# The neighbourhood layer of a four-layer attention network: 19x19 surroundings instead of three row blocks

## The chip, the cores and the metric

The kernel runs on one core of a Trainium2 chip. The metric is the device time of one execution in microseconds (us). The core's engines are PE (TensorE, matrix products, with PEld for its weight loads), DVE (VectorE), ACT (ScalarE), POOL (GpSimd) and SP (SyncE, which here only issues DMAs). They run independent instruction streams in order and wait for each other through semaphores. PSUM is the memory that PE writes to, in banks of 512 float32 per partition; SBUF is the on-chip memory of all engines.

## What is computed

Eight images of 32x32 tokens with 192 channels run through four layers. Each normalises its input over channel groups, applies attention with 12 heads of 16 channels and adds the outcome to its input. Layers 0 and 2 add relative positions to the scores, layer 3 rotates q and k and adds a 5x5 convolution of v. Layer 1, the only one that the change touches, lets a query see the 7x7 tokens around it (moved inwards at the border) and 16 register tokens that all queries share:

```python
mask = make_neighbourhood_mask(7, 7, h, w)              # rows start_h..start_h+6 and columns start_w..start_w+6
mask_cat = jnp.concatenate([mask, jnp.ones((s, r), dtype=bool)], axis=-1)
scores = jnp.einsum('bnqe,bnke->bnqk', q, k_cat) * scale
scores = jnp.where(mask_cat[None, None], scores, NEG_INF)
attn = jax.nn.softmax(scores, axis=-1)
o = jnp.einsum('bnqk,bnke->bnqe', attn, v_cat)
return o.reshape(n, h, w, nh * e) @ out_w.T + out_b
```

`start_h` is `clip(h_pos - 3, 0, 25)`, so a query in the upper half of the image sees key rows 0 to 18 only, one in the lower half rows 13 to 31; columns likewise.

## The kernel before

`program` runs the layers one after another. For layer 1 it calls `normalise_block` and then `attend_block` with kind "window"; each is a block of its own, and the engines meet at its end.

`normalise_block` goes over the eight images: SP loads one (L126, L137), DVE takes statistics (L165) and writes the normalised image (L188), ACT writes input plus output bias (L259, L260), SP stores both (L141, L148). PE does one tiny product per image.

`attend_block` has 24 units: three groups of four heads, and in each the eight images. A unit has 32 tiles, a tile being 128 queries (four image rows, a chunk) of one head. The keys of a chunk are the 384 tokens of three neighbouring chunks and a block of 128 that holds the 16 registers and is masked otherwise: 512 keys (`KEYS_W`). Per tile

- `scores` (L782): q and k split into bf16 parts stacked to 96 rows, two products of 384 and 128 columns into one of four banks of `S`;
- `row_max` (L962, DVE): adds the mask, writes the negated sum to `PROB`, and its row maximum to `nmax`;
- `exponential` (L1043, ACT): exp of that tile in SBUF, with the row sum;
- `turn` (L799, PE): four 128x128 transposes into `PT`, then a copy of 512 columns to `PTS`, of even tiles by DVE (L973), of odd ones by ACT (L1054);
- `output` (L814, PE, once in four tiles): 16 products with V.

In the same streams, at fixed places t of the 32 tiles, stand the projections of the next unit's q, k and v (`job`, L445 and L460, all through the one PSUM bank `M`; DVE takes them out at L527, POOL splits q and k into three bf16 parts, SP moves these through DRAM into `KK` and `QQ`), and the tail of the last unit (`tail`: row sums inverted, spread and turned at L834, multiplied at L942, output projection at L843, copy at L1034, added to the stream in DRAM by POOL's DMA at L710). PE does not go on to the next job or tail before the last one's use of `M` is over (`prep_out`, `tail_out`). The loops over units are real loops for units 2 to 21, and every engine executes its instructions in the written order.

Rows of other layers are used below as prices. `attend_rot` (layer 3) has 96 units of eight steps, four heads and 256 queries each: per step eight transposes (L2402), ACT's exp straight out of PSUM (L2533) and a product of V in four column groups (L2413); every other step four score products (L2388); and a tail of a sum (L2425), an inverse (L2431) and the projection. `attend_rel` (layers 0 and 2) makes scores with rounded float32 operands (`F32R`) that occupy 64 of the array's 128 rows, in pairs (L1499, L1503, L1518, L1524).

## Time and profile before

| | us |
|---|---|
| runs without profile, median of three | 9050.09 |
| lowest and highest of them | 9038.95, 9065.04 |
| the profiled execution, own time | 9057.34 |
| its span, first to last instruction | 9055.6 |

The profiled execution lies 7 us above the median of the others. All times of the trace count from its first instruction. A view of instructions gives for a group its count and busy time; PE's durations contain the length of its pipeline, so that n products in a row take about n times their spacing plus one latency. "Idle before" names what released the engine. A stage in this text is one block of one layer. A float32 product appears as two records in the trace, each with its own weight load, a transpose and a rounded float32 (`F32R`) product as one.

### The profile page before, as it was taken

Reading aid. Unit: us, or ns where it says so; the run is one execution under the profiler, and the core shown is the slowest. Engines: PE = TensorE matmul, PEld = TensorE weight load, DVE = VectorE, ACT = ScalarE, POOL = GpSimd, SP = SyncE. Lnnn points to the kernel's source line nnn. Section 1 sums busy time; section 2 is a strip of 40 time slices with the busy share of each in tenths; the row PEclk is TensorE's granted clock in tenths of the full one; section 3 lists DMA queues with packets and bytes.
Section 4 is the critical chain, followed back from the end, with each engine's and each line's share of the span. In section 5 each row is a group of like instructions: output and inputs, shape, how many; then the busy total and the mean of one; then the engine's idle time right before and its main releaser. Section 6 shows DMA issues by size and latency. Waiting matters only on the chain. (4 is left out here: it accounts for less than half of the span.)

```text
span 9055.6 us, 188790 instructions
## 1 busy us (share of the span) xinstructions
PE 7343.7 (81%) x62744; PEld 4481.5 (49%) x62744; DVE 5241.4 (58%) x8043; ACT 4335.9 (48%) x8449; POOL 2240.3 (25%) x2715
## 2 busy tenths in 40 slices
PE   2999999989388777846998999899556499999998
PEld 2555555555155555534555555555222255555555
DVE  3655555556255555553555555555588666666665
ACT  1444444444265656541444444445111277777776
POOL 2343434343121211214343434332111000000000
PEclk7989999999698999976998999899777799999999
DMA  6757666766433334346767565764312254445443
GB/s 160 134 114 142 124 131 119 138 120 112 110 74 70 74 68 76 69 119 117 142 119 129 115 135 117 132 121 82 101 56 80 78 133 112 122 119 127 116 119 90
DMA packets 536711, 999.82 MB, mean 110 GB/s; under 512 B 102258, under 2 KB 303027, under 8 KB 500211
## 3 DMA queue, kind: packets, MB, share of 16 engines
q1 hardware_dynamic: 479346, 900.50, 45.7%
q0 software_dynamic: 56576, 88.90, 6.5%
q8 instruction: 484, 7.93, 0.4%
q14 instruction: 305, 2.49, 0.1%
HBM read 645.95 MB, written 335.81 MB: 108 GB/s over the span
## 5 line engine op out<-in xcount | busy, mean ns | idle before, releaser
L1676 DVE TENSOR_REDUCE a_nmp<-a_S 128x2 f32<-128x1024 f32 x1536 | 1878.2, 1224 | 1362.7 <-PE a_S L1524 1347.3
L1777 ACT ACTIVATE a_PROB<-a_T 128x512 f32<-128x512 f32 x3072 | 1667.6, 595 | 1959.9 <-PE a_T L1503 1949.0
L1373 POOL CAST a_RF<-a_RL 32x512 fp32r<-32x512 f32 x1536 | 1295.0, 843 | 1120.8 <-DVE a_RL L1704 1028.8
L2492 DVE CUSTOM_DVE_ANT_0 a_X<-a_S,a_mask 128x1024 f32<-128x1024 f32 x768 | 910.0, 1223 | 551.9 <-PE a_S L2388 548.5
L1499 PE MATMUL a_T<-a_QW,a_KW 64*128 64x512 f32 x3072 | 813.4, 522 | 300.4 <-issue 135.3
L2533 ACT ACTIVATE a_PROB<-a_T 128x512 f32<-128x512 f32 x1536 | 835.8, 601 | 382.9 <-PE a_T L2402 382.9
L1499 PEld LDWEIGHTS a_T<-a_QW,a_KW 64*128 64x128 f32 x3072 | 313.8, 193 | 1312.3 <-issue 1309.3
L1537 PE MATMUL a_O<-a_PROB,a_V 128*32 128x512 f32 x6144 | 929.5, 681 | 2.5 <-ACT a_PROB L1777 2.5
L2402 PE MATMUL a_T<-a_ident,a_X 128*128 128x128 f32 x6144 | 824.7, 277 | 101.8 <-DVE a_OSB L2509 98.1
L962 DVE CUSTOM_DVE_ANT_0 a_PROB<-a_S,a_mask 128x512 f32<-128x512 f32 x768 | 522.8, 688 | 591.9 <-PE a_PT L799 498.4
L2402 PEld LDWEIGHTS a_T<-a_ident,a_X 128*128 128x128 f32 x6144 | 671.8, 141 | 303.0 <-issue 285.3
L1524 PEld LDWEIGHTS a_S<-a_KV,a_QV 64*128 64x128 f32 x6144 | 662.2, 203 | 124.2
L1518 PE MATMUL a_S<-a_KW,a_QW 64*128 64x512 f32 x3072 | 674.6, 427 | 55.1 <-issue 28.5
L1524 PE MATMUL a_S<-a_KV,a_QV 64*128 64x256 f32 x6144 | 667.2, 293 | 0.0
L1503 PE MATMUL a_T<-a_QV,a_KV 64*128 64x512 f32 x3072 | 657.9, 416 | 0.0
L2553 ACT ACTIVATE a_X<-a_X,a_rmax 128x512 f32<-128x512 f32 x768 | 564.6, 735 | 57.6 <-DVE a_rmax L2492 57.6
L1043 ACT ACTIVATE a_PROB<-a_PROB,a_nmax 128x512 f32<-128x512 f32 x768 | 550.5, 720 | 77.7 <-DVE a_nmax L962 77.7
L2343 POOL DMA_DIRECT2D out<-a_Y x96 | 92.0, 959 | 1805.0 <-ACT a_PROB L2533 1794.8
L799 PE MATMUL a_PT<-a_ident,a_PROB 128*128 128x128 f32 x3072 | 487.7, 283 | 50.4 <-ACT a_PROB L1043 30.3
L1564 PE MATMUL a_T<-a_QC,a_tab_d 16*32 16x64 f32 x6144 | 413.0, 300 | 138.3 <-issue 103.4
L2413 PE MATMUL a_O<-a_PROB,a_V 128*32 128x256 f32 x6144 | 491.1, 391 | 15.7 <-ACT a_OSB L2541 11.3
L2146 DVE SCALAR_TENSOR_TENSOR n_CV<-n_VP,n_lw,n_CV 96x1024 f32<-96x1024 f32 x384 | 461.0, 1275 | 0.0
(158 smaller groups left out, 9847.0 us busy)
## 6 DMA issues: line engine op xcount, KB each, us to landing
a_QV<-a_part_rows SPq DMA_DIRECT2D x384, 256.0 KB, 7.2
a_rel_rows<-a_RF SPq DMA_DIRECT2D x96, 1024.0 KB, 9.2
a_K<-part_rows SPq DMA_DIRECT2D x576, 128.0 KB, 4.0
a_X<-xn_scratch SPq DMA_DIRECT2D x72, 768.0 KB, 6.7
stream<-a_Y POOLq DMA_DIRECT2D x288, 192.0 KB, 4.6
a_part_rows<-a_part SPq DMA_DIRECT2D x48, 1024.0 KB, 12.2
a_QV<-a_part_rows SPq DMA_DIRECT2D x384, 128.0 KB, 7.8
a_QV<-a_rel_rows SPq DMA_DIRECT2D x384, 128.0 KB, 6.4
```

The lines of the kernel that those rows point to most:

```text
L1373: nc.gpsimd.tensor_copy(dst, src).then_inc(permuted, 1)
L1499: nc.tensor.matmul(T[:, slot(("st", s, pr, sd))], KW[lines, keys], QW[lines, par, pr, cols], start=True, stop=False)
L1503: nc.tensor.matmul(T[:, slot(("st", s, pr, sd))], KV[lines, par, pr, keys], QV[lines, par, pr, kc // 2, cols], start=False, stop=True).the ...
L1518: nc.tensor.matmul(S[:, pr, sd], QW[lines, par, pr, queries], KW[lines, kh * BANK:(kh + 1) * BANK], start=True, stop=False)
L1524: last = nc.tensor.matmul(S[:, pr, sd, here], QV[lines, par, pr, 2 * kh + kq, queries], KV[lines, par, pr, keys], start=False, stop=kq == 1)
L1537: last = nc.tensor.matmul(O[Q * g:Q * g + Q], V[:, par, kc, g], PROB[:, s % PRING, g], start=kc == 0, stop=kc == CHUNKS - 1)
L1676: nc.vector.tensor_reduce(nmp[:, qh, c, 2 * pr:2 * pr + 2, kh], S[:, pr], AX.X, ALU.max).then_inc(s_done, 1)
L1777: nc.scalar.activation(PROB[:, s % PRING, 2 * pr + sd], T[:, slot(("st", s, pr, sd))], ACT.Exp).then_inc(t_act, 1)
L2402: last = nc.tensor.transpose(T[:, slot(("t", kc, p)), P * (2 * sd + c):P * (2 * sd + c) + P], X[:, par, c, 2 * p + sd, P * kc:P * kc + P], ...
L2492: nc.vector.tensor_tensor_reduce(out=X[:, v % 2, c, g], in0=S[:, sd].rearrange("p a b -> p (a b)"), in1=mask[:, n % 2, g, c], scale=1.0, s ...
L2533: nc.scalar.activation(PROB[:, kc % PRING, 2 * p:2 * p + 2].rearrange("p g x -> p (g x)"), T[:, slot(("t", kc, p))], ACT.Exp, scale=-1.0). ...
L2553: nc.scalar.activation(here, here, ACT.Identity, scale=-1.0, bias=rmax[:, par, c, 2 * p + 1:2 * p + 2]).then_inc(x_act[half], 1)
```

## The change

`normalise_block` and `attend_block` are replaced, for layer 1, by `prepare_win` and `attend_win`; `attend_block` is gone. Layers 0, 2 and 3 keep their code.

The image is cut into quarters of 16x16 queries. A quarter's queries see only the 19x19 tokens in the corner of the image next to them. `prepare_win` goes over the images once. It normalises as before (DVE), then POOL gathers the four 19x19 surroundings with the registers in between into `XG` (4 x 384 tokens). PE projects q for all heads from the image and k and v from the gathered copy; q and k leave PSUM through DVE (bias, scale), ACT rounds them to `F32R`, DVE subtracts to get the rest, and SP stores both parts as `q_rows`, `k_rows`, `v_rows` in DRAM. The input is copied to the stream by eight DMAs from DRAM to DRAM. Everything is written out, without loops.

`attend_win` has 24 units again (four heads of one image), each with four quarters ("turns") of three key chunks of 128: 12 steps. A score is one `F32R` product over 79 rows: three times 16 rows of q and k parts, then 18 and 13 rows which hold the mask in factored form: one-hot rows on the query side for its place in rows and in columns, and on the key side 0 or -2^100; and two rows with the negated row maximum in two parts. Scores are made twice. Queries on partitions (`straight`), two tiles of 128 queries, four heads, only as many columns as these queries can see, for the row maximum, which DVE reads out of PSUM; and keys on partitions (`transposed`), 256 queries, for ACT's exp out of PSUM straight into `PROB`, so that nothing has to be transposed before the product with V. V has 16 columns of ones, which bring the row sums. The maxima are turned by PE two at a time (`turn_max`) and written by DVE into rows 64 and 65 of `Q_` (`take_max`).

```diff
-def attend_block(nc, sems, name, kind, xn, stream, w, ident):
+def attend_win(nc, sems, name, stream, w, ident, q_rows, k_rows, v_rows, near_lines):
+    UNITS = GROUPS * IMAGES
+    QUADS, CHUNKS_N = 4, NEAR // P
+    STEPS = QUADS * CHUNKS_N
+    RING, PRING, BUFS = 3, 3, 3
+    ROWS = 3 * DIM + 16 + 2 + 13
+    SPANS = {(0, 0): (0, 256, 0, 226), (0, 1): (94, 284, 0, 284), (1, 0): (0, 284, 0, 284), (1, 1): (128, 256, 24, 226)}
+    ITEMS = {0: (0, 1), 1: (2,), 2: (3,)}
+    TAIL = {2: "sum", 3: "turn0", 5: "turn1", 6: "wo00", 8: "wo01", 9: "wo10", 11: "wo11"}
+    NM_AT = 1
...
+            for u in range(UNITS):
+                for s in range(STEPS):
+                    quad, kc = divmod(s, CHUNKS_N)
+                    t = QUADS * u + quad
+                    transposed(u, s, 0)
+                    transposed(u, s, 1)
+                    if t + 2 < TURNS_N:
+                        for i in ITEMS[kc]:
+                            straight(t + 2, i)
+                    if s:
+                        values(u, s - 1)
+                    elif u:
+                        values(u - 1, STEPS - 1)
+                    if kc == NM_AT and t + 1 < TURNS_N:
+                        turn_max(t + 1)
+                    if u and s in TAIL:
+                        tail(TAIL[s], u - 1)
...
+            def row_max(t, i):
+                nc.vector.tensor_reduce(nm[:, t % 2, tile, 2 * pr:2 * pr + 2], S[:, n % 2, :, at:at + width], AX.X, ALU.max,
+                                        negate=True).then_inc(s_done, 1)
...
+            def take_max(t):
+                for g in range(G):
+                    last = nc.vector.tensor_copy(Q_[64:66, u % BUFS, g, WIDE * quad:WIDE * quad + WIDE],
+                                                 T[Q * g:Q * g + 2, slot(n), 0:WIDE])
...
+            def exponential(u, s, pr):
+                nc.scalar.activation(PROB[:, (STEPS * u + s) % PRING, 2 * pr:2 * pr + 2].rearrange("p g x -> p (g x)"),
+                                     T[:, slot(n)], ACT.Exp).then_inc(t_act, 1)
...
-        normalise_block(nc, sems, f"n{i}", x, xn, streams[i], w["bo"], a["gavg"])
-        if kind == "rel":
+        if kind == "window":
...
+            prepare_win(nc, sems, f"n{i}", x, streams[i], w, a["gavg"], q_rows, k_rows, near_rows, near_lines)
+            attend_win(nc, sems, f"a{i}", streams[i], w, a["ident"], q_rows, k_rows, near_rows, near_lines)
+        else:
+            normalise_block(nc, sems, f"n{i}", x, xn, streams[i], w["bo"], a["gavg"])
             attend_rel(nc, sems, f"a{i}", xn, streams[i], w, a["ident"])
```

The work is new code rather than moved code, so the order of two engines shows it best. TensorE in the attention of layer 1, before, four tiles in the middle of a unit's tail (`a_S` scores, `a_PT` transposes, `a_O` the product with V, `a_M` the output projection):

```order
L799 MATMUL a_PT<-a_ident,a_PROB 128x128 x4
L843 MATMUL a_M<-a_OSB,a_wo 96x512
L782 MATMUL a_S<-a_KK,a_QQ 128x384
L782 MATMUL a_S<-a_KK,a_QQ 128x128
L799 MATMUL a_PT<-a_ident,a_PROB 128x128 x4
L814 MATMUL a_O<-a_PTS,a_V 16x128 x16
L782 MATMUL a_S<-a_KK,a_QQ 128x384
L782 MATMUL a_S<-a_KK,a_QQ 128x128
L799 MATMUL a_PT<-a_ident,a_PROB 128x128 x4
L843 MATMUL a_M<-a_OSB,a_wo 96x512
```

The same engine now, three steps of a unit with two parts of the tail (`a_T` from `a_Q`,`a_K` the turned scores, `a_S` the straight ones, `a_T` from `a_nm_wide` the turned maxima):

```order
L798 MATMUL a_T<-a_Q,a_K 128x256 x4
L784 MATMUL a_S<-a_K,a_Q 128x256 x4
L813 MATMUL a_O<-a_PROB,a_V 32x256 x4
L847 MATMUL a_T<-a_OSB,a_wo 96x512
L798 MATMUL a_T<-a_Q,a_K 128x256 x4
L784 MATMUL a_S<-a_K,a_Q 128x284 x2
L813 MATMUL a_O<-a_PROB,a_V 32x256 x4
L823 MATMUL a_T<-a_ident,a_nm_wide 128x128 x2
L798 MATMUL a_T<-a_Q,a_K 128x256 x4
L784 MATMUL a_S<-a_K,a_Q 128x284 x2
L813 MATMUL a_O<-a_PROB,a_V 32x256 x4
L847 MATMUL a_T<-a_OSB,a_wo 96x512
```

The transposes of the probabilities are gone; each group of turned scores stands before the straight scores of two turns later and the product with V of the step before.

VectorE in the same stage, before: the masked maximum of each tile (its two rows are one call) and the copies of turned tiles.

```order
L962 ISA a_PROB,a_nmax<-a_S,a_mask 128x512
L962 ISA a_nmax 128x1
L973 COPY a_PTS<-a_PT 128x512
L962 ISA a_PROB,a_nmax<-a_S,a_mask 128x512
L962 ISA a_nmax 128x1
```

VectorE now, one turn and the start of the next:

```order
L887 TENSOR_REDUCE a_nm<-a_S 128x2 x3
L903 CAST a_Q<-a_T 2x256 x4
L887 TENSOR_REDUCE a_nm<-a_S 128x2
L893 CAST a_nm_hi<-a_nm 128x8
L895 COPY a_nm_wide<-a_nm_hi 128x8
L896 TENSOR_TENSOR a_nm_wide<-a_nm,a_nm_hi 128x8
L911 RECIPROCAL a_inverse<-a_T 128x32
L913 COPY a_inverse_wide<-a_inverse 128x1024
```

It has four reductions of two heads, four casts of two partitions and three small operations per turn, and the inverse of the row sums once in a unit.

## Rows read from the trace of the kernel before

**Rows 1.** The page's first line and its list of engines over the span.

```profile
span 9055.6 us, 188790 instructions
PE 7343.7 (81%) x62744; PEld 4481.5 (49%) x62744; DVE 5241.4 (58%) x8043; ACT 4335.9 (48%) x8449; POOL 2240.3 (25%) x2715
```

**Rows 2.** Timeline (start, us, operation): layer 1 begins, last store, attention begins, layer 2.

```profile
2360.21 0.34 SPq L121 DMA_DIRECT2D n_bias<-L_bo  x1
...
2435.75 0.32 SPq L148 DMA_DIRECT2D stream<-n_stream  x1
...
2442.78 0.37 SPq L577 DMA_DIRECT2D a_ident<-ident  x1
...
3985.64 0.34 SPq L121 DMA_DIRECT2D n_bias<-L_bo  x1
```

**Rows 3.** Stretch, length, busy time of each engine (count), TensorE's granted clock, DMA share, GB/s.

```profile
2360.00:2443.00 83.00, 3.83 (x16) 3.16 (x16) 40.99 (x113) 17.49 (x16) 5.62 (x9) 0.50 0.73 228
2443.00:2492.00 49.00, 20.27 (x40) 7.55 (x41) 3.49 (x9) 2.76 (x7) 8.47 (x12) 0.50 0.46 93
2492.00:3976.00 1484.00, 1199.28 (x12081) 778.44 (x12079) 844.84 (x2177) 906.73 (x2202) 286.46 (x396) 0.93 0.37 70
...
6383.00:7160.00 777.00, 415.62 (x1040) 192.44 (x1040) 612.64 (x660) 88.07 (x144) 98.20 (x68) 0.71 0.24 76
7160.00:9055.00 1895.00, 1687.16 (x14976) 1055.65 (x14976) 1248.88 (x2208) 1352.03 (x2496) 92.03 (x96) 0.99 0.48 118
```

**Rows 4.** Uses of the tile a_mask: ns min/median/max, first and last start in us.

```profile
L962 DVE CUSTOM_DVE_ANT_0 a_PROB<-a_S,a_mask x768: 679/691/693, 2491.2 to 3963.2; 128x512 f32<-128x512 f32 x192
L2492 DVE CUSTOM_DVE_ANT_0 a_X<-a_S,a_mask x768: 1219/1223/1225, 7182.0 to 9026.0; 128x1024 f32<-128x1024 f32 x192
```

**Rows 5.** Costliest groups from 2492 to 3976: busy us, mean ns, idle before and releasers.

```profile
L962 DVE CUSTOM_DVE_ANT_0 a_PROB<-a_S,a_mask 128x512 f32<-128x512 f32 x767 | 522.1, 688 | 576.2 <-PE a_PT L799 498.4 <-PE a_S L782 57.7 <-issue 19.8
L799 PE MATMUL a_PT<-a_ident,a_PROB 128*128 128x128 f32 x3072 | 487.7, 283 | 50.4 <-ACT a_PROB L1043 30.3 <-DVE a_PTS L973 16.6 <-issue 1.9
L445 PE MATMUL a_M<-a_X,a_wv 96*64 96x512 f32 (+1 forms) x276 | 129.5, 600 | 109.2 <-DVE a_whole L527 109.2
L843 PE MATMUL a_M<-a_OSB,a_wo 128*96 128x512 f32 x192 | 100.9, 607 | 62.5 <-DVE a_OSB L942 61.7 <-ACT a_Y L1034 0.8
```

**Rows 6.** Timeline of PE in layer 0's attention: start, busy us, operation, count.

```profile
1503.25 0.39 PE L1518 MATMUL a_S<-a_KW,a_QW 64*128 64x512 f32 x2
...
1503.48 0.40 PE L1524 MATMUL a_S<-a_KV,a_QV 64*128 64x256 f32 x4
...
1503.80 1.98 PE L1545 MATMUL a_T<-a_X,a_wqk 96*128 96x512 f32 x4
...
1505.72 0.50 PE L1499 MATMUL a_T<-a_QW,a_KW 64*128 64x512 f32 x2
```

**Rows 7.** Timeline of layer 3's attention: start, busy us, operation, count.

```profile
8001.92 0.64 PE L2413 MATMUL a_O<-a_PROB,a_V 128*32 128x256 f32 x8
...
8002.49 1.09 PE L2402 MATMUL a_T<-a_ident,a_X 128*128 128x128 f32 x8
...
8008.77 0.61 PE L2425 MATMUL a_T<-a_pick,a_OSB 128*128 128x4 f32 x4
```

**Rows 8.** Groups by line over the whole span, as prices for DVE and ACT.

```profile
L1676 DVE TENSOR_REDUCE a_nmp<-a_S 128x2 f32<-128x1024 f32 x1536 | 1878.2, 1224 | 1362.7 <-PE a_S L1524 1347.3
L2533 ACT ACTIVATE a_PROB<-a_T 128x512 f32<-128x512 f32 x1536 | 835.8, 601 | 382.9 <-PE a_T L2402 382.9
...
L2509 DVE TENSOR_TENSOR a_OSB<-a_OSB,a_T 128x256 f32<-128x256 f32 x96 | 39.9, 415 | 2.9 <-PE a_T L2431 2.9
...
L1683 DVE CAST a_nm_hi<-a_nm 128x16 fp32r<-128x16 f32 x96 | 29.6, 309 | 3.3
```

**Rows 9.** Timeline at the start of layer 3's preparation: first load, first large product.

```profile
6383.28 0.34 SPq L1926 DMA_DIRECT2D n_X<-stream  x1
...
6404.19 9.81 PE L2023 MATMUL n_T<-n_XN,n_wv 96*96 96x512 f32 x16 [3.30 <-DVE n_XN L2095]
```

More of the change, by code:

```diff
@@ L469, in add_v_jobs @@
-        def add_v_jobs(step, halves):
-            for i, half in enumerate(halves):
-                job(step + 2 * i, project(wv_sb, G * DIM, half), act=[v_out(half)])
-                run, place = turn_v(half)
-                job(step + 2 * i + 1, run, act=[place])
-        def free_whole(n, piece):
-            before = UNIT_STEPS * n + SPLIT_STEPS * piece - (REL_STEPS if piece == 0 else 0)
-            need(nc.vector, split, before, solo=True)
-            if rel:
-                need(nc.vector, moved, 16 * G * (PIECES * n + piece), solo=True)
@@ L571, in attend_block @@
+        CONSTS = 16 * (len(const) + 1)
+        SETUP = 5
+        NORM = 10
+        GATHERS = 2 * QUADS
         block = ctx.enter_context(nc.Block())
@@ L785, in turn @@
-            def turn(u, t):
-                T = TILES * u + t
-                pe.wait_ge(exp_done, T + 1)
-                for h in range(TURNS):
-                    bank = t % 2 if window else h
-                    if window:
-                        need(pe, evac_act if t % 2 else evac_dve, EVACS * u + t // 2)
-                    else:
-                        need(pe, evac_act if h else evac_dve, T)
-                    alone(pe)
-                    for j in range(4):
-                        k = BANK * h + P * j
-                        last = nc.tensor.transpose(PT[:, bank, P * j:P * j + P], PROB[:, t % PROBS, k:k + P], ident_sb[:])
-                    last.then_inc(turned, 1)
@@ L903, in _ @@
+            pe.wait_ge(consts_loaded, CONSTS)
+            pe.wait_ge(set_up, SETUP)
+            alone(pe)
+            mean(0)
+            for b in range(IMAGES):
+                for i, n in enumerate(ORDER):
+                    job(b, n)
+                    if i == FIRST_MEAN and b + 1 < IMAGES:
+                        mean(b + 1)
         @block.vector
         def _(eng):
-            def scale_k(n):
-                eng.wait_ge(loaded, 16 * LOADS * (n + 1))
-                for ap in scaled:
-                    last = nc.vector.tensor_scalar(ap, ap, SCALE, None, ALU.mult)
-                last.then_inc(w_scaled, 1)
@@ L1018, in _ @@
+            rest(NP * IMAGES - 1)
         @block.scalar
         def _(act):
[L1020 to L1034 removed]
@@ L1081, in epilogue, with high @@
-            def epilogue():
-                n = UNITS - 1
-                outputs(n, 1)
-                tail(n, 1, 1)
-                tail(n, 1, 2)
-            pairs(act, prologue, body, epilogue)
+            act.wait_ge(consts_loaded, CONSTS)
+            act.wait_ge(set_up, SETUP)
+            alone(act)
+            def high(n):
+                b, i = divmod(n, NP)
+                what, m, at = PIECES[i]
+                act.wait_ge(t_dve, n + 1)
+                if at == 0:
+                    need(act, (q_stored if what == "q" else k_stored)[m], 16 * b)
+                alone(act)
+                if what == "q":
+                    ins = nc.scalar.copy(q_part[:, m, 0, at * BANK:(at + 1) * BANK], whole[:, n % BLOCKS])
+                else:
+                    ins = nc.scalar.copy(k_part[:, m, 0, at], whole[:, n % BLOCKS, 0:NEAR])
+                ins.then_inc(hi_done, 1)
@@ new lines, in values @@
+            def values(b, j):
+                s = b % 2
+                act.wait_ge(t_ready, done(b, ("v", j, 0), "pe"))
+                if j == 0:
+                    need(act, v_stored[s], 16 * (b // 2))
+                alone(act)
+                nc.scalar.copy(VT[:, s, 2 * j:2 * j + 2, :, 0:DIM],
+                               T[:, ORDER.index(("v", j, 0)) % RING, 0:2 * CHANNELS].rearrange(
+                                   "p (c h d) -> p c h d", c=2, d=DIM)).then_inc(t_act, 1)
+            for b in range(IMAGES):
+                for n in ORDER:
+                    if n[0] == "v":
+                        values(b, n[1])
+                    else:
+                        high(NP * b + PIECES.index(n))
```

1222 lines of the change are left out of this document (574 added, 648 removed).

## The prediction

> **What bounds the kernel now.** I read first the list of engines [rows 1]: TensorE (PE) is busy for 81% of the span and nothing else is near. That is an average over eight stages, and the change touches two, so the second view is the three starts [rows 2]: layer 1 runs from 2360.2 to 3985.6, 1625.4 us. Its normalisation takes 82.6 of them, its attention 1542.9. The third view is the table by stage [rows 3]. In the normalisation PE does nothing and DMA has a share of 0.73. In the first 49 us of the attention PE is at the lower clock. In the long stretch PE is busy for 1199 of 1484 us with a granted clock of 0.93, DVE for 845, ACT for 907.
>
> The use of the mask gives the period: 768 tiles in 1472 us, 1.92 us a tile, 61.4 us a unit [rows 4]. The groups say who waits: DVE sat idle 498 us until PE's transposes were over [rows 5]. PE in turn waited 109 us at the v projection for DVE to empty the only bank `M`, and 62 us at the output projection for the product in `OSB` [rows 5]. So PE's in-order stream ends last: its work, plus handovers in the stream. The prices below give 1.7 us of PE work a tile (four transposes 0.56, two score products 0.4, a quarter of the V product 0.25, projections and tail 0.5) against 1.92. What counts for the change is PE's work per unit.
>
> **Prices of PE records at 2.4 GHz.** A float32 product of 512 columns: four records from 1503.80 to 1505.72 [rows 6], less 0.2 for the change of group, 0.43 each, 0.84 ns a column. A rounded float32 product: a pair of 512 columns in the two halves of the array passes in 0.23 (1503.25 to 1503.48), and four of 256 in 0.32 as two pairs (to 1503.80) [rows 6]; so 0.115 for 256 columns and 0.1 for a change of group. The V product of layer 3 (four column groups, 256 columns, two records each) takes 0.57 with its change (8001.92 to 8002.49) [rows 7]; the new one has the same shape. A transpose: (1.09 - 0.28)/7 = 0.116, with the 283 ns of one as latency [rows 5, 7]. A product of four columns, where only the weight load counts: (0.61 - 0.26)/3 = 0.117, with about 0.26 for one, my estimate [rows 7].
>
> The new scores take 79 rows, so they can't run in pairs side by side: each of them pays its 0.115 alone. The Trainium skill ("TensorEngine Tiling (Array Packing)", Key Properties) has a rule against the new order: a change of tiling mode drains the engine, and each step goes from the full array to 32-column groups and back. By the row the whole V group, change included, is 0.57, of which 0.43 are its columns, so no more than 0.14 is lost [rows 7]. The sum would be 0.2 us a step more if a drain of a whole latency came at each change; layer 3's row has both changes in it and doesn't show that.
>
> **Attention, per step.**
> - Turned scores: 4 x 0.115 and two changes, 0.66.
> - Straight scores: 8/3 products of 256 or 284 columns at 0.12 and a change, 0.42.
> - V product 0.57. Two transposes of maxima in three steps, 0.11.
> - Tail per unit: sum 16 x 0.117 = 1.87, turns 8 x 0.116 = 0.93, projection 8 x 0.43 = 3.44, seven changes 0.7; 6.94/12 = 0.58.
>
> Together 2.34 us. The same prices on layer 3 give 2.24 (transposes 1.13, V 0.57, scores 0.28, tail 0.26); measured are 95 units of eight steps in 1844 us, 2.43 [rows 4]. A finished pipeline of this kind thus loses 0.19 a step to handovers and to its clock (0.99 [rows 3]); with 0.11 for the new one, whose DVE and ACT are less loaded, I take 2.45 us. Bounds: 2.25 if the changes of group cost less and no wait is left, 2.9 if the waits double those of layer 3 and the clock is granted at 0.93 as now [rows 3]. The work of 288 steps: 706 us (648 to 835).
>
> Does another engine end later? ACT: two exps of 512 columns at 0.60 [rows 8], a third of an output copy of 256 columns and a third of a projection copy of 512, which by their columns cost 0.3 and 0.6 like an exp: 1.5. DVE per turn: four reductions of 452 or 568 elements. By elements of the 1024-wide one (1.22) they cost 0.61, by a fixed share at most 0.75: 2.4 to 3.0. Four casts of two partitions by 256: no row shows them; between the 0.31 of a 16-element cast and the 0.42 of a 256-wide product from PSUM, 1.2 to 1.7 [rows 8]. The small split 0.9. With a tail of 2.3 a unit that is 1.7 to 2.05 a step. Both lie under 2.45, and hide behind PE. If PE were faster than 2.05, DVE would be next. The dangerous wait is take_max: after PE turns two maxima, DVE has 1.7 us of casts, and PE comes to the turned scores that need them one step (2.4) later. PE would stand 0.3 us or so a turn if casts took 0.6. DMA: 2.7 MB of operands and 0.8 MB of stream per 29 us, 120 GB/s, as in layer 3 (118 at share 0.48 [rows 3]), issued two units ahead: hidden.
>
> **Preparation, per image.** q: 32 records of 256 columns, 6.9 us; k: 32 of 384, 10.3; v: 72 of 192, 11.6; 18 changes of group 1.8. That is 30.7 us of PE, 31 with the tiny product of the means, at full clock. It replaces 10 us an image of normalisation and takes the projections out of the attention. DVE has about 21 us (statistics and normalisation 5.1 as now, 40.99 us for eight images [rows 3], then 12 copies out of PSUM and 12 subtractions at 0.5 to 0.8), ACT 9, POOL some 5 for the gathers, which start 8 us before their use. The stores and loads are 7.1 MB an image, at the 228 GB/s of the normalisation [rows 3] 31 us too; its share was 0.73, so 23 us if more is possible. So 31 us (29 to 38), eight images 248 (232 to 304).
>
> Around it: from first load to first large product 20.9 us in layer 3's preparation [rows 9]; I take 21, since the memsets of POOL are of the same size. After the last product 9 us of evacuation and stores, and 8 of block change (now 7 between the last store at 2435.75 and 2442.78 [rows 2]). Start of the attention: 18 constant loads, then operands, the first scores and maxima, 27. End: last tail, last store and block change 25, where now 22 lie between the last masked maximum (3963.2 [rows 4]) and the next layer.
>
> **Sum.** 21 + 248 + 17 + 27 + 706 + 25 = 1044 us against 1625.4 [rows 2]: 581 saved. Layers 0, 2 and 3 keep their time. The span 9055.6 becomes 8475, the profiled execution 9057.3 becomes 8476, and on the median's base 9050.1 - 581 = 8469; I say 8470.
>
> **Rivals.**
> 1. Handovers and DVE decide (12%): casts on two partitions cost 0.6, PE stands for the maxima, a step takes 2.85. For it: it is the one chain through PE, DVE and PE with one step of air. Against: DVE has 0.4 to 0.7 us a step to spare. 288 x 0.4 = 115 more: 8585.
> 2. The preparation runs at the lower clock (7%): in all short stages of now the grant is 0.50, in layer 3's preparation 0.71 [rows 3]. For it: PE there waits for ring slots and for the next image. Against: these stages have PE busy for 5 to 53% of the time, here it would be dense. At 1.2 GHz 30 us an image more, 240: 8710.
> 3. No waits left (5%): 2.2 us a step, 8398.
> 4. Slower than before (3%): both new stages stay at the lower level for good. The 40% busy first 49 us of the attention had it [rows 3]. The preparation pays 240, a step of 2.34 becomes 4.7, 288 x 2.25 = 648 more: 9358. The point from which it decides is a step of 4.47 us, with the preparation as forecast; with the preparation at 1.2 GHz 3.6 us. Against it: 0.93 and 0.99 in the two stages with PE as busy as here.
> 5. DMA bounds the preparation (3%): 36 to 40 us an image, 8530.
> That the transposes stay in some form is excluded by the order of instructions: none of `PROB` is left.
>
> **Chances.** My forecast, step 2.3 to 2.65 and image 29 to 35 us, has 70%; its own range is 8410 to 8560. The range for 8 in 10 takes in rival 3 and 5 and most of 1, and the bounds of step (-58, +129) and image (-16, +56): low 8390, high 8640. Rival 2 and 4 stay out. A difference of 0.3%, 27 us, is what a measurement of this kernel can tell from none. Faster by more than that: all but rival 4, 97%. Within it 1%, slower 2 to 3%.
>
> **What would show it.** In the changed profile the layer starts at 2360 and ends near 3404. PE's products with V in it should come 2.45 us apart, 29 us a unit; waits of the turned scores for `a_Q` casts would show rival 1; DVE busy under 2 us a step. In the preparation q's first products come every 31 us and the clock is above 0.9; below 0.7 is rival 2; idle of DVE or ACT on `q_rows`, `k_rows` or `v_rows` is rival 5. Wrong from the start would be the prediction if a product of 79 rows in `F32R` has not the 0.115 us of a paired one: at twice that a step takes 3.1 us, 8660.

## The result, and the profile after

The changed kernel takes 8731.6 us (median of four, 8712.5 to 8750.1) against 9046.4 us before: a ratio of 0.965, interval 0.9632 to 0.9666. It is faster by 315 us, as forecast in sign; forecast were 580 us, and the time lies above the range's end of 8640. The profiled execution took 8719.0 us, its span 8717.3. Of the 338 us between the two spans 291 are layer 1; the rest lies in code that did not change.

The page of the kernel after, its first line and its engines, answers [rows 1]:

```profile
span 8717.3 us, 168356 instructions
PE 7201.7 (83%) x56896; PEld 4389.3 (50%) x56896; DVE 5013.6 (58%) x7203; ACT 3870.8 (44%) x7137; POOL 2200.3 (25%) x2407
```

PE's share has gone up and its work down by 142 us only. The starts of its four parts (timeline of the kernel after: start, busy us, operation) answer [rows 2]; the third row is the groups of turned scores, with their durations and first and last start:

```profile
2355.25 0.34 SPq L369 DMA_DIRECT2D n_X<-stream  x1
2789.18 0.34 SPq L711 DMA_DIRECT2D a_ident<-ident  x1
L798 PE MATMUL a_T<-a_Q,a_K x1152: 274/283/1202, 2853.1 to 3665.5; 79*128 79x256 f32 x192
3689.23 0.35 SPq L122 DMA_DIRECT2D n_bias<-L_bo  x1
```

Layer 1 now takes 3689.2 - 2355.3 = 1334 us where it took 1625.4 and was forecast at 1044. The missing 290 us are all in it. (What lies behind layer 1, unchanged code, took 5028 us against 5070 before; in the profiled executions of the twelve runs below that part lies between 5001 and 5055. Differences of that size are no effect of an edit, and the experiments are read from layer 1 first and from the whole time second.)

The stages (windows of the kernel after: stretch, length, busy time of PE, PEld, DVE, ACT, POOL with their counts, granted clock, DMA share, GB/s) answer [rows 3]. They are the preparation, the start of the attention, and its long stretch:

```profile
2355.00:2791.00 436.00, 354.83 (x1104) 218.04 (x1104) 152.29 (x305) 73.31 (x144) 49.92 (x85) 0.72 0.44 148
2791.00:2853.00 62.00, 5.09 (x18) 4.22 (x19) 6.02 (x14) 0.00 (x0) 0.00 (x0) 0.50 0.96 134
2853.00:3680.00 827.00, 712.78 (x5168) 464.63 (x5166) 505.05 (x1139) 388.31 (x768) 18.61 (x24) 0.87 0.52 99
```

Against the terms of the forecast, in us (an image is the spacing of the first `XN` of each, a step that of the first turned score of each, both from their starts in the trace):

| | forecast | after | too low by |
|---|---|---|---|
| preparation, to the first `XN` and product | 21 | 28 | 7 |
| eight images | 8 x 31 = 248 | 8 x 48.84 = 391 | 143 |
| end of it and block change | 17 | 15 | -2 |
| start of the attention | 27 | 63.9 | 37 |
| steps (288 forecast, 287 spacings measured) | 706 (2.45 each) | 811.9 (2.83 each) | 106 |
| end | 25 | 24 | -1 |

Three terms hold the miss, and each has waits in the trace that the prediction did not have. Waits of the preparation, DVE (who waits for what: us in all, times, longest):

```profile
DVE n_stats L514 <- DMA n_X<-stream: 82.5, 7, 12.2
DVE n_near_round L556 <- DMA n_near_drawn<-L_near: 37.0, 1, 37.0
```

The statistics of seven images wait some 12 us each for the image itself. The SP queue and DVE around one of them (timeline: start, busy us, operation, in brackets the idle time before):

```profile
2535.80 0.38 SPq L399 DMA_DIRECT2D near_rows<-n_VT  x1
2536.27 1.80 SPq L382 DMA_DIRECT2D n_X<-stream  x1
2552.81 2.47 DVE L514 BATCH_NORM_STATS2 n_stats<-n_X 96x6 f32<-96x512 f32 x4 [12.15 <-DMA n_X<-stream]
```

The load of the next image stands on SP behind the last store of the one before, is issued 0.5 us after it, and lands 16.5 us later. While DVE waits, PE runs dry, and what it does next is slow. A group of four records of the k projection in the first image and after the wait (PE's timeline):

```profile
2394.14 1.45 PE L485 MATMUL n_T<-n_XG,n_wk 96*96 96x384 f32 x4
2556.84 2.84 PE L485 MATMUL n_T<-n_XG,n_wk 96*96 96x384 f32 x4 [0.18 <-DVE n_whole L571]
```

At the start of the attention SP itself waits, with q and k of all units queued behind it; the second row is the median landing of one of its twelve loads of mask rows:

```profile
SPq L41 <- DMA a_K<-near_lines: 30.9, 1, 30.9
a_K<-near_lines SPq DMA_DIRECT2D x3, 360.0 KB, 21.9
```

In the steps, PE's waits from 2845 to 3660 are:

```profile
PE a_O L813 <- issue: 43.3, 71, 1.1
PE a_T L847 <- DVE a_Q L903: 26.1, 43, 0.9
PE a_O L813 <- ACT a_OSB L963: 17.3, 23, 0.8
PE a_T L834 <- DVE a_Q L903: 14.5, 23, 0.6
PE a_T L841 <- DVE a_Q L903: 7.5, 12, 0.6
...
PE a_T L798 <- DVE a_Q L903: 0.6, 1, 0.6
```

There are two waits in each turn: one at the V product, in part put down to ACT's copy of the output; and one of 0.6 us at whichever tail product stands at kc = 2 (the sum, turn 1, two projections), for the casts of `take_max`. The forecast's dangerous wait, turned scores for these casts, occurs once (last row). And the clock: 0.87 on average, but not evenly. PE in a unit with its tail (timeline; `L834` are the 16 records of the sum's eight products):

```profile
3120.45 0.64 PE L813 MATMUL a_O<-a_PROB,a_V 128*32 128x256 f32 x8 [0.75 <-ACT a_OSB L963]
3121.02 0.44 PE L823 MATMUL a_T<-a_ident,a_nm_wide 128*128 128x128 f32 x2
3121.21 0.72 PE L798 MATMUL a_T<-a_Q,a_K 79*128 79x256 f32 x4
...
3123.36 1.92 PE L834 MATMUL a_T<-a_pick,a_OSB 128*128 128x4 f32 x16 [0.63 <-DVE a_Q L903]
...
3127.68 1.20 PE L798 MATMUL a_T<-a_Q,a_K 79*128 79x256 f32 x4
```

and the windows around it: the sum alone, then 8 us behind it.

```profile
3123.30:3125.20 1.90, 1.83 (x17) 1.87 (x17) 1.00 (x4) 0.00 (x0) 0.00 (x0) 1.00 1.01 171
3126.00:3134.00 8.00, 7.78 (x48) 5.07 (x48) 5.62 (x13) 3.27 (x7) 0.00 (x0) 0.55 0.98 213
```

In the sum PE shows no gap and has the full clock. Soon after it the clock is at 1.2 GHz for most of 8 us, although PE is busy for 7.78 of them. Over the 24 units, the share of time at the lower level by step (0 to 11) is 0.04, 0.04, 0.15, 0.59, 0.65, 0.48, 0.33, 0.16, 0.12, 0.04, 0, 0: it starts behind the sum in step 2 and is under 0.2 from step 7 on.

### The profile page after: what moved, and what is told of

It is laid out like the page before. It is cut to its first block and busy times, and to the rows that moved or that the text cites. A ratio compares the mean times of both kernels' runs of the same rounds, so it can differ in the third digit from the quotient of the medians.

```text
span 8717.3 us, 168356 instructions
## 1 busy us (share of the span) xinstructions
PE 7201.7 (83%) x56896; PEld 4389.3 (50%) x56896; DVE 5013.6 (58%) x7203; ACT 3870.8 (44%) x7137; POOL 2200.3 (25%) x2407
## 5 line engine op out<-in xcount | busy, mean ns | idle before, releaser
L1681 ACT ACTIVATE a_PROB<-a_T 128x512 f32<-128x512 f32 x3072 | 1667.6, 595 | 1924.8 <-PE a_T L1407 1911.8
L2437 ACT ACTIVATE a_PROB<-a_T 128x512 f32<-128x512 f32 x1536 | 835.7, 601 | 382.2 <-PE a_T L2306 382.2
L954 ACT ACTIVATE a_PROB<-a_T 128x512 f32<-128x512 f32 x576 | 323.9, 597 | 371.3 <-PE a_T L798 371.3
L1468 PEld LDWEIGHTS a_T<-a_QC,a_tab_d 16*32 16x32 f32 x6144 | 359.1, 125 | 184.4 <-issue 166.8
L1608 DVE TENSOR_TENSOR a_RL<-a_T,a_RL 128x512 fp32r<-128x512 f32 x192 | 132.5, 690 | 452.3 <-ACT a_RL L1698 452.2
```

Of the source, the lines that this page charges most:

```text
L1468: last = nc.tensor.matmul(T[at + 32:at + 64, to, 64 * a:64 * a + 64], tab_d[:, x], QC[:, :, half * BANK + x:(half + 1) * BANK:SIDE], start ...
L1681: nc.scalar.activation(PROB[:, s % PRING, 2 * pr + sd], T[:, slot(("st", s, pr, sd))], ACT.Exp).then_inc(t_act, 1)
L2437: nc.scalar.activation(PROB[:, kc % PRING, 2 * p:2 * p + 2].rearrange("p g x -> p (g x)"), T[:, slot(("t", kc, p))], ACT.Exp, scale=-1.0). ...
```

## Experiments

Each kernel has the changed kernel as its base. Ratios are against the kernel before on the same chip; the changed kernel has 0.965. "The clock" of a stretch is the mean granted clock as a share of 2.4 GHz, 0.5 being 1.2 GHz throughout.

### The load of the next image

```diff
+            sp.dma_start(X[:, 1], x_in[1]).then_inc(x_loaded[1], 16)
...
-                if b + 1 < IMAGES:
-                    need(sp, xn_ready, 2 * b)
+                if b + 2 < IMAGES:
+                    sp.wait_ge(xn_ready, 2 * b + 2)
                     alone(sp)
-                    sp.dma_start(X[:, (b + 1) % 2], x_in[b + 1]).then_inc(x_loaded, 16)
+                    sp.dma_start(X[:, b % 2], x_in[b + 2]).then_inc(x_loaded[b % 2], 16)
```

> The preparation's load of the next image but one is issued as soon as its buffer is free, ahead of the stores of q, k and v, instead of behind the stores of the image before. Theory (the load waits in the queue behind 5.9 MB of stores, DVE waits for it, and PE with DVE): DVE's wait for n_X falls from 82.5 us to under 5, an image takes 31 to 37 us instead of 49.0, the granted clock of the stage rises from 0.72 to over 0.85, and the kernel gets 85 to 140 us faster than the changed kernel (8732), to about 8620. Rival (the DMA engines are full, the stores only wait elsewhere): DVE or ACT wait for q, k or v stores instead, an image stays over 44 us, the gain is under 35 us. Second rival (the clock stays low although the wait is gone): an image takes 42 to 45 us, gain 30 to 50 us.

Measured: 8600.9 us, 0.950 (0.9473 to 0.9522). The preparation took 315.3 us instead of 433.9, an image 33.1. Its window, beside the one of the kernel after above:

```profile
2350.00:2667.00 317.00, 272.15 (x1104) 174.54 (x1104) 153.26 (x305) 74.77 (x144) 51.88 (x85) 0.93 0.60 203
```

No wait of the statistics is left. The load itself is no faster: it still stands behind a `v_rows` store and lands after 16.5 us (median), but it is now issued an image ahead of its use. The same 1104 records of PE take 272 us instead of 355: 83 of the 119 us are the clock (0.72 to 0.93), which the wait had cost in addition to itself. DMA moves 203 GB/s in this window instead of 148, so its rate had not been the limit (rival 5).

### What lowers the clock in a unit

The first kernel makes the row sums for two of the eight chunks of queries only, each with its four columns four times, and leaves the other six out, so its row sums are wrong.

```diff
-                    for c in range(CHUNKS):
-                        last = nc.tensor.matmul(T[:, to, G * c:G * c + G], OSB[:, o, P * c:P * c + P], pick_sb[:],
+                    for c in range(2):
+                        last = nc.tensor.matmul(T[:, to, 16 * c:16 * c + 16].rearrange("p (r g) -> p r g", g=G), OSB[:, o, P * c:P * c + P],
```

> Left out: six of the eight products that bring the row sums to the other side in each unit; the two that stay write 16 columns each, so that all other steps run as before with wrong sums. 24 units lose 12 records of 0.117 us, 34 us. Theory (the 1.9 us of full weight loads with four columns behind them bring PE's clock down for the steps behind): the share of the lower clock in steps 3 to 6 of a unit, now 0.33 to 0.65, falls below 0.2, the clock of the stage rises from 0.87 to over 0.93, a unit gets 3 us or more shorter, the kernel 70 to 100 us faster than 8732. Rival (the clock follows the waits or the mix of the whole stage): it stays at 0.87, the gain is 30 to 40 us.

Measured: 8644.9 us, 0.954 (0.9523 to 0.9554). A step takes 2.52 us, the clock of the steps is 0.971, and steps 3 to 6 are at the lower level for 4% of their time. But work was removed with it: 12 of 16 records, 1.3 us in each of 23 units, some 31 of the 89 us by which the steps became shorter.

The second kernel keeps all of the work and gives it more: the same eight products move their four columns sixteen times, 64 columns each.

```diff
-                        last = nc.tensor.matmul(T[:, to, G * c:G * c + G], OSB[:, o, P * c:P * c + P], pick_sb[:],
-                                                start=True, stop=True)
+                        last = nc.tensor.matmul(T[:, to, 64 * c:64 * c + 64].rearrange("p (r g) -> p r g", g=G), OSB[:, o, P * c:P * c + P],
+                                                pick_sb[:].unsqueeze(1).to_broadcast([P, 16, G]), start=True, stop=True)
```

> The eight products of the row sums keep their weights and their number, but each moves 64 columns instead of 4 (the four wanted ones repeated 16 times); DVE reads the first four of each 64. Nothing is left out. Weight loads still set their pace (0.117 us a record), so the stretch stays at 1.9 us. Theory that the clock falls because almost no columns move in this stretch: the share of the lower clock in steps 3 to 5 falls below 0.25, clock of the stage over 0.93, step 2.55 to 2.7 us instead of 2.83, 40 to 80 us faster than the changed kernel (8732 to 8746 by its ratio). Rival (it falls because of the stretch's length with nothing but weight loads, or the 0.6 us wait in front): share stays at 0.6, time within 10 us.

Measured: 8638.0 us, 0.954 (0.9518 to 0.9554); step 2.63, clock 0.972. PE in a unit of this kernel, the sum and the second turned scores behind it:

```profile
3076.78 1.97 PE L834 MATMUL a_T<-a_pick,a_OSB 128*128 128x64 f32 x16 [0.63 <-DVE a_Q L903]
...
3080.72 0.72 PE L798 MATMUL a_T<-a_Q,a_K 79*128 79x256 f32 x4
```

The sum takes nearly as long as before (1.97 against 1.92, although sixteen times the columns pass), the wait before it is the same 0.63, and the turned scores that took 1.20 take 0.72. PE waits as often as before at the V product and more often for the casts (90 times instead of 78). So neither the wait nor the sum's length by itself lowers the clock: the two kernels differ in how many columns pass behind each weight load, 4 or 64, and only the one with 4 loses it. Numbers between were not tried. It is worth 0.203 x 287 = 58 us in the steps. (Layer 1 is 71 us shorter and the whole time 94; 11 of it came from the preparation, which this edit doesn't touch.) The Trainium skill ("TensorE: Matmul & The Clock Gate", Part 1) says the gate goes by how busy PE has recently been; by the trace's busy time the two kernels are the same there, and only one loses its clock, so the busy time of a profile does not tell which will.

A way around it without wider products is to make the sum in two parts, in steps 0 and 2:

```diff
-    TAIL = {2: "sum", 3: "turn0", 5: "turn1", 6: "wo00", 8: "wo01", 9: "wo10", 11: "wo11"}
+    TAIL = {0: "sum0", 2: "sum1", 3: "turn0", 5: "turn1", 6: "wo00", 8: "wo01", 9: "wo10", 11: "wo11"}
```

> The eight products of the row sums in two parts of four, in step 0 (first half of the tokens) and step 2 of a unit, with their own inverses. PE's work is the same. If the clock falls because of one long stretch of weight loads, two of 0.9 us with dense products between leave it up: share of the lower clock under 0.2 everywhere, step 2.5 to 2.6, 65 to 90 us faster than the changed kernel. If what counts is how much of such work a unit has, the share stays near 0.2 on the average, and the time within 20 us.

Measured: 8752.0 us, 0.965 (0.963 to 0.9679); step 2.91, clock 0.83, share at the lower level 0.23, 0.37, 0.63, 0.7, 0.6, 0.45 in steps 1 to 6. Half the stretch is enough to lose the clock, and there are two of them. The gain that was expected from shorter stretches did not come; the time is that of the changed kernel, as the other case had it.

### ACT's copy of the output

ACT copies the output of a turn after the first exp of step kc = 1. It goes to kc = 0, behind both exps:

```diff
                     exponential(u, s, 0)
-                    if s % CHUNKS_N == 1 and t:
-                        outputs(t - 1)
                     exponential(u, s, 1)
+                    if s % CHUNKS_N == 0 and t:
+                        outputs(t - 1)
```

> ACT copies the finished output of a turn one step part earlier, right behind the exps in whose step PE finishes it, instead of behind the next step's first exp. PE's first product with V of a turn then has nothing to wait for. Theory (these waits are on the path): the 0.75 to 0.9 us before the first V product of each of 96 turns go, 50 to 75 us faster than 8732, steps 1 of each turn 2.0 us instead of 2.5 to 2.9. Rival (PE then waits elsewhere, for the casts of the maxima): under 20 us.

Measured: 8642.0 us, 0.954 (0.9496 to 0.9574). A step takes 2.53 us; the steps with kc = 1 fell from medians of 2.50, 2.91, 2.89 and 2.80 to 1.67, 2.51, 2.00 and 2.00. PE's waits from 2850 to 3577, all rows there are:

```profile
PE a_T L847 <- DVE a_Q L903: 21.3, 45, 0.6
PE a_T L834 <- DVE a_Q L903: 13.7, 22, 0.6
PE a_T L841 <- DVE a_Q L903: 13.1, 21, 0.6
```

All waits at the V product are gone, those of "issue" too: 71 and 23 in the list above are 94, about one for each turn, so the row "issue" was the same wait. The edit is worth 0.296 x 287 = 85 us, more than the 60.6 us of these waits, and the waits for the casts stayed at 48. The rest came with the clock (0.894 over the steps instead of 0.871, some 55 us less at the lower level, which by its half speed is worth up to 27). Steps 3 and 4 are still at the lower level for 0.59 and 0.68 of their time, so this wait is not what lowers the clock; but in steps 5 and 6 the share fell from 0.48 and 0.33 to 0.13 and 0.08, so without the wait the clock comes back sooner. The V product waits for the copy of the turn before because the two turns use the two halves of one bank (`O` is 2 x 256 float32); what a bank for each would bring was not tried.

### The casts of the maxima and the ring slot

`turn_max` takes one of three slots of `T`, and it is free again after four casts. The tail product that stands behind it at kc = 2 needs that slot. Here the tail goes ahead of the maxima, and all of its parts but the last to kc = 0 or 1; DVE's stream follows the same order:

```diff
-    TAIL = {2: "sum", 3: "turn0", 5: "turn1", 6: "wo00", 8: "wo01", 9: "wo10", 11: "wo11"}
+    TAIL = {3: "sum", 4: "turn0", 6: "turn1", 7: "wo00", 9: "wo01", 10: "wo10", 11: "wo11"}
...
-                    if kc == NM_AT and t + 1 < TURNS_N:
-                        turn_max(t + 1)
                     if u and s in TAIL:
                         tail(TAIL[s], u - 1)
+                    if kc == NM_AT and t + 1 < TURNS_N:
+                        turn_max(t + 1)
```

> Six of the seven parts of the tail stand in the first and second step of a turn, ahead of the turned maxima, so that they no longer wait for the ring slot that the four casts of the maxima hold. Theory (this slot is the wait at the tail in every third step): PE's waits for the casts (26 + 14.5 + 7.5 us, and the same time again in weight loads) go, 25 to 45 us faster than 8732, more if the clock rises. Rival (PE comes to the turned scores that need the casts sooner and waits there): the same time is lost in front of the turned scores, gain under 10 us or a loss of up to 30.

Measured: 8775.0 us, 0.967 (0.9635 to 0.9706); step 3.04, clock 0.776: the steps behind the sum are at the lower level for 0.91, 0.98 and 0.96 of their time. The casts' waits fell from 48 us to 15, and the loss of clock took more: the time rose by 43 us, beyond both expectations. Why the clock falls deeper here than in the changed kernel stays open. It says nothing yet on the order itself; that comes below, on a base where the clock holds.

### The two starts

DVE rounds the mask rows after the first image's normalisation instead of before, and the mask rows are loaded buffer by buffer, each ahead of the unit that needs it:

```diff
             eng.wait_ge(consts_loaded, CONSTS)
-            nc.vector.tensor_copy(near_round[:], near_drawn[:]).then_inc(near_rounded, 1)
             statistics(0)
...
             normalise(0)
+            eng.wait_ge(near_stored, 16)
+            nc.vector.tensor_copy(near_round[:], near_drawn[:]).then_inc(near_rounded, 1)
...
-            for s in range(BUFS):
+            def mask_rows(s):
                 for lines, n, at in ((y_rows, 16, 0), (x_rows, 15, 16)):
...
-                    sp.wait_ge(consts_loaded, CONSTS)
+                    mask_rows(s)
+                    sp.wait_ge(consts_loaded, CONSTS + 16 * 4 * s)
```

> The rows of the mask are rounded and stored after image 0 is normalised, and the attention's three buffers get their mask rows one after the other, each followed by its operands, so that the first unit waits for four of the twelve row loads and its own operands alone. Expected from the trace of the changed kernel: first normalised image 21 us after the stage's begin instead of 28, first turned scores 30 to 40 us after the attention's begin instead of 64; together 30 to 40 us faster. Rival (all loads share the same engines and the first unit waits for the sum of them): first turned scores still after 50 us, gain under 20 us.

Measured: 8710.4 us, 0.962 (0.9587 to 0.9657). The first `XN` comes 16.8 us after the start instead of 28.0, the first turned scores 40.8 us after the start of the attention instead of 63.9: 34 us in the two, which is what the trace shows. The whole time fell by 21, and the two intervals of the ratio overlap, so it does not show the gain clearly. The first q and k now go out 16.3 us after the start of the attention, the first straight scores come 15.7 us later, and from there to the first turned scores it is 8.8 us.

### All of it

The first kernel has the early image, the early copy, the sum in two parts and the two starts.

> The early load of the images, the early copy of outputs, the sums in two parts and the later mask rows together. If their causes are apart the gains add: 137 for the image load, 85 to 100 for the copy, 65 to 90 for the sums, 30 to 40 for the starts, of which the clock's share can be won once only: step 2.2 to 2.3 us, layer 1 about 1040 to 1080 us instead of 1336, the kernel at 8420 to 8490. If they overlap (the copy's waits and the sum's stretch bring the clock down together) the step stays at 2.4 and the kernel over 8500.

Measured: 8473.0 us, 0.936 (0.9345 to 0.9376); layer 1 takes 1071.7 us, a step 2.46 at a clock of 0.93. The time is as expected for gains that add, the step is not (2.2 to 2.3 expected): PE still waits 48 us for the casts, and the clock is not full. The second has the wide sum in place of the one in two parts:

> The early load of the images, the early copy of outputs, the later mask rows and the sums with 64 moving columns in one part. Theory (the short columns of the sums are what brings the clock down, and nothing else in this stage does): low share under 0.1 in all steps, clock 0.97, step 2.40 us, which is the mean of the steps 0 to 11 as the runs with the early copy and with wide columns each had them; layer 1 1050 to 1070 us, the kernel at 8440 to 8470. Rival (the early copy makes another stretch light and the clock falls there): step over 2.5, no faster than 8473.

Measured: 8432.6 us, 0.930 (0.9282 to 0.9313). It computes everything and is the fastest of those that do. Layer 1 takes 1054.8 us: 304.5 for the preparation, 41.1 for the start of the attention, 686.4 for the steps (2.39 each, clock 0.96) and 23 for the end.

On this base the tail was moved ahead of the maxima, with the same edit as above:

> As the kernel with all four and wide sums, and six of the seven parts of the tail before the turned maxima, as in the run in which that alone cost time. Theory (there it lost only through the clock, and the wait for the ring slot that the casts hold is real, 0.4 to 0.6 us in four steps of a unit): with the clock up it gains 1.2 to 2 us a unit, step 2.25 to 2.3, the kernel 30 to 45 us faster than its companion. Rival (the turned scores then wait for the casts instead): the same time within 10 us, PE idle before the turned scores.

Measured: 8458.4 us, 0.933 (0.9315 to 0.9348), a step 2.43. The clock now stays (0.968), and the order brings nothing (26 us more than its companion, 12 of them in the steps): the waits go to the turned scores, which take the same slots one place later. The longest of PE's waits in this kernel:

```profile
PE a_T L803 <- DVE a_Q L908: 25.2, 46, 0.6
PE a_T L803 <- ACT a_Y L982: 9.7, 28, 0.4
PE a_T L803 <- DVE a_OSB L924: 9.5, 23, 0.4
```

The last pair asks what the casts still cost, by making only the first of the four, beside the same kernel with all of them. Three heads of four then subtract stale maxima, and the result is wrong:

```diff
-                for g in range(G):
+                for g in range(1):
                     last = nc.vector.tensor_copy(Q_[64:66, u % BUFS, g, WIDE * quad:WIDE * quad + WIDE],
```

> All the edits of e9_all_wide, and of the four casts that store the maxima's two rows of the four heads only the first is made; the rows of the other three heads stay as they were, so three heads of four subtract wrong maxima. It asks what the casts still cost when the rest is mended: four of them take about 1.7 us a turn on VectorE, one takes 0.43, so each turn has 1.3 us less between the reductions and the next products that want their slot. Theory (the casts are the last wait left on the way): TensorE's waits before the turned scores, the tail products and the weight-load products for a_Q go, and the step falls from 2.39 to about 2.2, some 45 us less than e9_all_wide. Rival (TensorE's own work and its handovers from line to line are what is left): the step stays within 0.05 us of 2.39 and the time within 15 us of e9_all_wide.

> The same kernel as e9_all_wide, on the same chip as e11_one_cast, so that the two are compared side by side: 8433 us within 20, step 2.39 us.

Measured: 8410.8 us (0.929, 0.9261 to 0.931) with one cast, 8434.5 us (0.933, 0.9304 to 0.9356) with four; a step takes 2.227 against 2.392. PE's waits in the stretch of the steps, first with four casts (the first three rows), then with one (all rows there are):

```profile
PE a_T L852 <- DVE a_Q L908: 20.5, 44, 0.5
PE a_T L846 <- DVE a_Q L908: 14.1, 23, 0.6
PE a_T L839 <- DVE a_Q L908: 13.7, 22, 0.6
```

```profile
PE a_S L789 <- DMA a_Q<-near_lines: 4.9, 1, 4.9
PE a_T L803 <- issue: 1.4, 1, 1.4
PE a_S L789 <- issue: 0.5, 1, 0.5
PE a_O L818 <- issue: 0.4, 1, 0.4
```

The 48.3 us of waits are gone and the steps are 47.3 us shorter: the theory holds in the trace. The tail products read nothing that the casts write, so what they waited for is the slot. The whole time fell by 24 us only, between the two expectations; in the profiled executions layers 2 and 3 took 54 us more than in the kernel beside it (5054.7 against 5000.6), which is as far apart as that part ever was. The window of the steps with one cast shows what is left:

```profile
2701.00:3335.00 634.00, 626.85 (x5081) 410.44 (x5081) 379.85 (x849) 388.81 (x753) 17.35 (x22) 0.95 0.69 132
```

PE is busy for 99% of it, at a clock of 0.95. 2.2 us a step is PE's own work.

## Why the prediction was right and wrong

**Right: the sign, PE's prices and what hides behind PE.** Where no wait falls and the clock is full, steps 0, 3, 6 and 9 of the kernel after take 2.06, 2.16, 2.23 and 2.55 us (medians), and with nearly all waits removed the mean of all steps is 2.23, against a sum of prices of 2.34. The 79-row product is not twice the price of a paired one: four with their changes take the 0.56 from 3121.21 to the next group at 3121.77, forecast were 0.66. The drain at each change of tiling mode, which would have made it 2.54, is in no row. (The price of being wrong there was set too low: twice the time for both kinds of scores adds 0.46 + 0.32 us, a step of 3.2 and about 8690, not 3.1 and 8660.) DVE's reductions took 0.63 and 0.75, as bounded, its work is 1.75 us a step (505 us in 288 steps), ACT's 1.35; both hide. DMA hides behind the steps (share 0.52). End and block change were right within a microsecond or two.

**Wrong: the image, 31 us, measured 48.8.** The work was right: with the load early an image takes 33.1. The failed step is the bound on transfers, "The stores and loads are 7.1 MB an image, at the 228 GB/s of the normalisation [rows 3] 31 us too; its share was 0.73, so 23 us if more is possible". That was a rate; what counted was the place of one load in SP's order. `x_in[b + 1]` stands behind the `v_rows` store of image b - 1, and that store waits for the last of ACT's work on it. So the load is issued when its image is already due, and lands behind a store of 2.3 MB after 16.5 us. The Trainium skill ("DMA: Bandwidth & Descriptors", Queues, rings and completion order) says that on each DMA engine the descriptors of a queue are consumed in ring order; the trace agrees: the load issued 0.5 us behind that store, whose own median landing is 14.0 us, lands last. It would have been enough to walk SP's order in the kernel. PE's gaps that go with it are 36 us in all (436.0 - 354.8 against 317.0 - 272.2); rival 2 came on top of it, for the reason that the forecast named ("PE there waits for the next image") and then set aside with the word "dense". The clock was 0.72, as in layer 3's preparation (0.71 [rows 3]), the nearest row; for the full clock that the forecast took there was no row. It cost 83 us, a third of rival 2's price, since the clock came back within each image.

**Wrong: the start of the attention, 27 us, measured 63.9.** It was costed as a count of loads. The twelve loads of mask rows (3.7 MB) hold up SP for 30.9 us before the first q and k go out. DMA in that stretch (window of the kernel after):

```profile
2792.00:2828.00 36.00, 0.00 (x0) 0.00 (x0) 0.00 (x0) 0.00 (x0) 0.00 (x0) 0.50 0.95 112
```

It moves 112 GB/s at a share of 0.95, so the 228 GB/s of [rows 3] was not a price for them. Loads for buffers that are needed two units later have no business in front; apart they cost 23 us less. The remaining 41 against 27 are 16.3 us for the constants and four mask rows, 15.7 for the operands of one unit and 8.8 for its first scores and maxima, one behind the other; how the forecast's 27 divides among them it did not say.

**Wrong: the step, 2.45 us, measured 2.83.** The term that failed is the 0.11 for handovers and clock. Measured in its place:

| | us a step | from |
|---|---|---|
| PE's own work | 2.23 (2.34 forecast) | one cast on the mended base |
| casts hold the slot of the tail | 0.165 | one cast against four |
| V product waits for ACT's copy | 0.296 | copy early |
| clock behind the sum | 0.203 | wide sum |

The sum of it is 2.89, 0.06 more than was there: with both the copy early and the sum wide a step falls by 0.437 and not by 0.296 + 0.203, since the early copy alone already brings a part of the clock back. Three mistakes are in it. First, the copy: it stood behind an exp of turned scores that PE makes only in the same step, while the V product that PE comes to next in that step needs it; "hide behind PE" was said of ACT's total, not of the one instruction that PE waits for. Second, rival 1 had the right engines but the wrong place: casts took 0.42 each, the upper end of the bound, at which the forecast saw no wait. It would have been none for the turned scores of the next turn; the one that waits is the tail product in the step between, for the slot. The forecast looked at who needs the data and not at who needs the buffer. Third, the clock: the tail of layer 3 has a sum of four records [rows 7], and its stage keeps 0.99 [rows 3]; the new one has sixteen. The price per record was right (0.12); that sixteen in a row lower the clock of the five steps behind them was in no row of the kernel before, and busy time does not show it.

Put together: with everything mended but the casts, layer 1 takes 1055 us against the forecast of 1044, and the whole 8433 us where 8470 was forecast, since the layers around it took less than in the execution that the forecast started from. That this lies so near is in part luck: PE's work came 0.11 us a step below its price and the waits for the casts 0.165 above nothing, an image takes 33.1 instead of 31 and the start of the attention 41 instead of 27, against the first image, which comes 4 us sooner than forecast. The forecast described the kernel that this change could be, and not its queues. The 8 in 10 range had 29 to 38 us for an image from DVE, DMA and PE one by one; no end of it came from an order of instructions.

## What to carry to other kernels

- Work and rates give a floor; for each stage also walk each queue once, SP's too, and ask of every load which store it stands behind, and of every product whose buffer it takes, not only whose data. The load, the copy and the slot were all to be read from the order of instructions.
- An engine that is hidden in the sum can still hold the bound one by a single instruction in the wrong place. Moving ACT's copy of 0.37 us ahead of one exp was worth 85 us.
- A wait in front of PE can have a second price, the clock of what follows: in the preparation it was larger than the wait (83 against 36 us); in the steps the wait for the copy cost 61 us and some 24 more, because the clock came back later.

## What the runs showed of the hardware

- Sixteen records with full weight loads and four columns each (1.92 us, no gap, full clock) are followed by 1.2 GHz for most of 8 us of busy PE; with 64 columns each they take 1.97 us and are not. With two groups of eight the clock falls as well (0.829 over the steps against 0.871).
- A cast from PSUM to two partitions of 256 rounded floats takes 0.42 us (415 to 429 ns). A product of 128 partitions by 256 from PSUM took 0.415 [rows 8], so the few partitions saved nothing against it.
- With loads of mask rows (15 or 16 partitions each) in flight, the DMA share was 0.95 at 112 GB/s; in a window with stores and loads of whole images it was 0.60 at 203 GB/s. Here the share says nothing of the rate.
- The unchanged layers behind layer 1 took 5001 to 5055 us in the twelve profiled executions, 1%. A gain of 20 us needs the trace of its own stage.
